# A new slot order for the attention stacks, with merged rotary products

## The reference, cut to what matters

```python
for i in range(DEPTH):                                    # 6
    x = attn_layer(shift_tokens(x), Wqkv[i], ...) + x
    x = ffn_layer(shift_tokens(x), ln_g[i], ...) + x
# attn_layer: 16 heads of 64, window 32
q, k, v = split(x @ Wqkv)
q = l2norm(q) * qs;  k = l2norm(k) * ksc
q = q * cos * scale + rotate_half(q) * sin * scale        # k with 1 / scale
sim = einsum(q, k of this window and the one before) * 8; masked
out = softmax(sim) @ v;  out @ Wo
# ffn_layer: layer norm, a * gelu(gate) @ W2 + b2, inner width 341
```

## Time and profile before

| | us |
|---|---|
| median of 3 runs | 4334.24 (4328.81 to 4348.74) |
| profiled execution | 4352.9 |
| its span in the profile | 4351.2 |
| TensorE busy | 4027.8 (93%) |
| VectorE busy | 3345.6 (77%) |
| ScalarE busy | 3100.0 (71%) |
| GpSimd busy | 1798.7 (41%) |
| mean of one factor (L835) | 1.469 |
| mean of one addition (L841) | 2.364 |
| mean of one exponential (L1143) | 0.363 |

### The profile page before, as it was taken

One profiled execution on the slowest core, in us unless ns is written; L12 is line 12 of the kernel. 1 busy time (PEld: TensorE's weight loads), 2 busy tenths in 40 slices (PEclk: granted clock), 3 DMA queues, 4 the chain that ended last, 5 costly groups with the idle time before them and its releaser, 6 DMA issues. The chain is left out here.

```text
span 4351.2 us, 113662 instructions
## 1 busy us (share of the span) xinstructions
PE 4027.8 (93%) x43857; PEld 2388.8 (55%) x43857; DVE 3345.6 (77%) x4981; ACT 3100.0 (71%) x7032; POOL 1798.7 (41%) x1071
## 2 busy tenths in 40 slices
PE   7997999999999999999967689999999999999998
PEld 3443555555555555555536545555555555555554
DVE  5774888888888888888735478888888888888885
ACT  3555777777777777777762267777777778777776
POOL 3111444444444444444404534444444444444442
PEclk7997999999999999999986589999999999999999
DMA  2212444444443443444300044444434444444342
GB/s 44 31 21 70 95 111 102 99 101 101 105 111 90 111 107 90 111 99 103 84 10 3 3 107 109 101 97 109 110 87 115 102 100 100 102 105 111 92 100 52
DMA packets 232520, 380.78 MB, mean 88 GB/s; under 512 B 59364, under 2 KB 122336, under 8 KB 231688
## 3 DMA queue, kind: packets, MB, share of 16 engines
q1 hardware_dynamic: 231560, 372.20, 36.9%
q10 hardware_dynamic: 384, 0.79, 0.1%
HBM read 39.22 MB, written 1.05 MB: 9 GB/s over the span
## 5 line engine op out<-in xcount | busy, mean ns | idle before, releaser
L835 POOL TENSOR_TENSOR b_prob<-b_prob,b_rinv 128x768 f32<-128x768 f32 x384 | 564.3, 1469 | 1778.3 <-DVE b_rinv L1281 1778.3
L841 POOL TENSOR_TENSOR b_prc<-b_prc,b_sws 128x1024 f32<-128x1024 f32 x384 | 907.7, 2364 | 72.2 <-DMA b_sws<-b_prs 72.2
L1143 ACT ACTIVATE b_prob<-ps,b_nmx 128x96 f32<-128x96 f32 x3072 | 749.0, 363 | 0.0
L885 PEld LDWEIGHTS ps<-ident,b_prob 128*128 128x128 f32 x3072 | 367.9, 140 | 406.5 <-ACT b_pT L1079 232.8
L1216 DVE SCALAR_TENSOR_TENSOR b_prc<-ps,b_qks,b_rot 128x512 f32<-128x512 f32 x768 | 571.1, 744 | 14.0 <-ACT b_sq L1104 13.3
L1218 DVE SCALAR_TENSOR_TENSOR b_prs<-ps,b_qks,b_rot 128x512 f32<-128x512 f32 x768 | 570.1, 742 | 0.0
L885 PE MATMUL ps<-ident,b_prob 128*128 128x128 f32 x3072 | 513.0, 281 | 46.5 <-DVE b_kr L1264 37.1
L1262 DVE TENSOR_TENSOR b_prc<-b_prc,ps 128x512 f32<-128x512 f32 x384 | 263.6, 686 | 369.9 <-PE ps L950 288.3
L1079 ACT ACTIVATE b_pT<-ps 128x512 f32<-128x512 f32 x724 | 435.5, 601 | 154.1 <-PE ps L885 151.1
L987 PE MATMUL ps<-b_wqkv,b_xs 128*128 128x256 f32 x1536 | 435.0, 406 | 2.2 <-DVE b_prs L1218 2.2
L938 PE MATMUL ps<-b_xs,b_wqkv 128*128 128x512 f32 x768 | 408.9, 614 | 23.3 <-issue 10.0
(11 more groups left out here) (293 smaller groups left out, 7218.0 us busy)
## 6 DMA issues: line engine op xcount, KB each, us to landing
b_sws<-b_prs SPq DMA_DIRECT2D x1536, 128.0 KB, 2.3
b_vs<-b_va SPq DMA_DIRECT2D x384, 256.0 KB, 3.8
b_wqkv<-in_L_ffn_Wqkv SPq DMA_DIRECT2D x96, 192.0 KB, 3.6
b_xs<-y SPq DMA_DIRECT2D x126, 128.0 KB, 2.3
b_wo<-in_L_ffn_Wo SPq DMA_DIRECT2D x96, 64.0 KB, 3.1
b_xs<-y SPq DMA_DIRECT2D x42, 127.8 KB, 2.4
b_rot<-in_rot SPq DMA_DIRECT2D x2, 2048.0 KB, 7.8
b_w<-in_L_ffn_W SPq DMA_DIRECT2D x24, 170.5 KB
```

The lines of the kernel that those rows point to most:

```text
L835: pool.tensor_tensor(prob[:, r, :, P - KEYS:P], prob[:, r, :, P - KEYS:P], rinv[:, r % 2, :].rearrange("p (b a) -> p b a", a=1).broadcast_ ...
L841: pool.tensor_tensor(prc[:, r, :, :], prc[:, r, :, :], sws[:, r % 2, :, :], ALU.add)\
L885: t = pe.transpose(bank[6][:, i * P:(i + 1) * P], prob[:, kd, 4 * e + 2 * h + m, :], ident[:, :])
L1143: g = act.activation(prob[:, kb, i, P - KEYS:P], wide[0][:, e * CH + m * KEYS:e * CH + (m + 1) * KEYS], ACT.Exp, bias=nmx[:, kb % 2, i:i + 1])
```

## The change

The order of the instructions of a slot is written anew for TensorE, ScalarE, VectorE and GpSimd; SyncE's stays. The special order after a gelu goes. Banks: the spreads use 1 and 2 (so the key projection waits for L1262, which empties bank 1), the strips bank 6, the output projection bank 7, mean, variance and gates bank 2, hidden and output products bank 3.

TensorE's slot becomes: first transposition (after the factor of its unit), output projection of the unit of age 5, spreads, query, hidden or output product of the feed-forward part, key, second transposition, mask and scores, strips (odd), values, mean, variance or gate, value projection. A `sem_inc` on a semaphore that nobody waits for is put ahead of mask and scores. GpSimd adds before it multiplies by the factor. VectorE starts a slot with the rotary products of the unit before, each pair of products one instruction; `prc`, `prs` and `kr` become parts of one tensor for that.

```diff
+        roll = sb("roll", [P, 12 * CH + PAD + T])
+        prc = roll[:, 0:8 * CH].rearrange("p (r i c) -> p r i c", r=4, i=2)
+        prs = roll[:, 8 * CH:12 * CH].rearrange("p (r i c) -> p r i c", r=2, i=2)
+        kr = roll[:, 12 * CH:12 * CH + PAD + T]
+        def two_runs(first, second):
+            return bass.AP(roll[:, :].tensor, first, [roll[:, :].ap[0], [second - first, 2], [1, CH]])
 # GpSimd
-                    if u: ... wait rinv_done ... pn_done      (the factor, moved down)
                     if v:
                         pool.wait_ge(S["swap_ld"], ONE + 64 * (U + 1))
                         ... add ... .then_inc(S["add_done"], 1)
+                    if u: ... wait rinv_done ... pn_done
 # TensorE, slot
+                    if d:
+                        pe.wait_ge(S["pn_done"], ONE + UD + 1)
+                        if p and j % 2 == 0:
+                            pe.wait_ge(S["ln_done"], ONE + twos(p) + 1)
+                        turn(UD, kd, 0)
+                    if e:
+                        pe.wait_ge(S["o_cp"], ONE + UE + 1)
+                        pe.matmul(bank[7], wo[:, pair(e), :], oT[:, ke % 2, :], ...).then_inc(S["wo_mm"], 1)
+                    if b:
+                        pe.wait_ge(S["split_done"], ONE + twos(b) + 1)
+                        if p:
+                            pe.wait_ge(S["pk_done"], ONE + um(p)[0] + 1)
+                        pe.matmul(bank[1][:, :], take[:, 2 * (kb % 2), :], rsp[:, :], ...)
+                        key_bank_free(f0)
+                        pe.matmul(bank[2][:, :], take[:, 2 * (kb % 2) + 1, :], rsp[:, :], ...).then_inc(S["nb_mm"], 1)
                     if a: ... query projection, behind va_cp ...
+                    hidden_bank_free(f0)
+                    ... hidden product (f_in) or output product (f_hid) into bank[3] ...
+                    if a:
+                        if b:
+                            pe.wait_ge(S["qn_done"], ONE + UB + 1)
+                        pe.matmul(bank[1][:, :], W[:, 1, :], X, ...).then_inc(S["k_mm"], 1)
+                    if d:
+                        turn(UD, kd, 1)
                     if b:
+                        pe.wait_ge(S["exp_done"], ONE + UB)
+                        pe.wait_ge(S["kn_done"], ONE + UB + 1)
+                        pe.sem_inc(S["s_go"], 1)
                         mask(kb) ... scores
+                    if a and j % 2:
+                        strips(U, d)               # waits sqk_done of U, pt_cp of both halves
                     if d:
                         values(d, 0)
                         values(d, 1)
+                    ... mean, variance or gate into bank[2], behind kn_done ...
                     if a: ... value projection, behind sqq_done and pq_done ...
 # ScalarE, slot: copy of output (e); square of step 1; variance or gate copy; copy of values (p);
 #   first transposition; affine of step 2; table load; exponentials (age 3); square of query;
 #   second transposition; table load and gelu (step 5); square of key; inverse norms (odd)
+                    if d:
+                        turned(1)
                     if step == 5:
                         act.preload_act_table_set("gelu_and_others")
                         act.wait_ge(S["f_gcp"], ONE + FT * C + FT)
                         act.activation(gel, gel, ACT.Gelu).then_inc(S["f_gelu"], 1)
+                    if a:
+                        act.wait_ge(S["k_mm"], ONE + U + 1)
+                        act.activation(sq[:, 2 * (r % 2) + 1, :], bank[1][:, :], ACT.Square).then_inc(S["sqk_done"], 1)
+                        if j % 2:
+                            inverse_norms(twos(a))
 # VectorE
-                    dve.scalar_tensor_tensor(out=prc[:, r, i, :], in0=bank[i][:, :], scalar=scale,
-                                             in1=rot[:, 2 * i, t], op0=ALU.mult, op1=ALU.mult)
-                    dve.scalar_tensor_tensor(out=prs[:, r % 2, i, :], in0=bank[i][:, :], scalar=scale,
-                                             in1=rot[:, 2 * i + 1, t], op0=ALU.mult, op1=ALU.mult).then_inc(S[done], 1)
+                    both = bank[i][:, :].rearrange("p (a c) -> p a c", a=1).broadcast_to([P, 2, CH])
+                    dve.scalar_tensor_tensor(out=two_runs((2 * r + i) * CH, (8 + 2 * (r % 2) + i) * CH), in0=both, scalar=scale,
+                                             in1=rot[:, 2 * i:2 * i + 2, t], op0=ALU.mult, op1=ALU.mult).then_inc(S[done], 1)
 # VectorE, slot: products of p (query, key); maximum (age 3); norm of step 2; centring; hidden copy;
 #   y of the feed-forward part; split (even); query rows (b); y (e); key rows (b); sum and reciprocal (age 3)
```

More of the change, by code:

```diff
@@ new lines, in slot @@
+                    if ok is not None:
+                        pe.wait_ge(S["f_hid"], ONE + OC + 1)
+                        for i in range(FT):
+                            m = pe.matmul(bank[3][:, :], w2[:, i, :], hid[:, i, :], start=(i == 0), stop=(i == FT - 1))
+                        m.then_inc(S["f_out"], 1)
+                    if a:
+                        if b:
+                            pe.wait_ge(S["qn_done"], ONE + UB + 1)
+                        elif p:
+                            pe.wait_ge(S["pk_done"], ONE + um(p)[0] + 1)
+                        pe.matmul(bank[1][:, :], W[:, 1, :], X, start=True, stop=True).then_inc(S["k_mm"], 1)
@@ L952, in slot @@
-                    if d and before != 5:
-                        turn(UD, kd, 0)
-                    key_bank_free(f0)
-                    if a:
-                        pe.wait_ge(S["pk_done"], ONE + U)
-                        pe.matmul(bank[1][:, :], W[:, 1, :], X, start=True, stop=True).then_inc(S["k_mm"], 1)
-                    if d and before == 5:
-                        turn(UD, kd, 1, b)
-                    if d and before != 5:
-                        turn(UD, kd, 1, b)
-                    if a and j % 2 and before != 5:
-                        strips(U, b)
@@ L989, in slot @@
                         m.then_inc(S["va_mm"], 1)
-                    if a and j % 2 and before == 5:
-                        strips(U, b)
-                    if d:
-                        if isinstance(d[0], int) and d[0] == 0:
-                            pe.wait_ge(S["wo_ld"], ONE + 16 * PAIRS * (L0 + 1))
-                        elif d[1] < HALF and d[1] % 2 == 0:
-                            pe.wait_ge(S["wo_ld"], ONE + 16 * (PAIRS * (L0 + d[0]) + pair(d) + 1))
-                        pe.wait_ge(S["o_cp"], ONE + UD + 1)
-                        if not b:
-                            pe.wait_ge(S["kn_done"], ONE + PER * (L0 + DEPTH))
-                        pe.wait_ge(S["y_add"], ONE + UD)
-                        pe.matmul(bank[3][:, :], wo[:, pair(d), :], oT[:, kd % 2, :], start=True, stop=True).then_inc(S["wo_mm"], 1)
@@ L1225, in slot @@
                     ok, OC = ffn_out(f0)
-                    follows = before in (0, 2, 4) or ok is not None
-                    if b and j % 2 == 0 and not follows:
-                        n = twos(b)
-                        dve.wait_ge(S["rn_done"], ONE + n + 1)
-                        dve.scalar_tensor_tensor(out=rsp[:, :], in0=rhi[:, :].bitcast(F32), scalar=minus_hi[:, 0:1], in1=rn[:, :],
-                                                 op0=ALU.mult, op1=ALU.add).then_inc(S["split_done"], 1)
```

278 lines of the change are left out of this document (122 added, 156 removed).

## The result

The changed kernel takes 4398.61 us, median of 4 runs (4395.76 to 4404.53), beside 4341.49 for the kernel before (4328.81 to 4351.09, 4 runs; the forecast was put on the 4334.24 of three): ratio 1.0135, 95% interval 1.0102 to 1.0168. It is 57 us slower, where 47 was forecast. The profiled execution spans 4402.8 us against 4351.2.

The account below looks back on a forecast made before the run. TensorE, busy 4027.8 of 4351.2 us, was taken as the bound; 22 half layers at 2.4 us more, less 2 x 3, gave 47 us on the 4334.24 median: 4381 us, range 4260 to 4465.

Parts of the forecast that it names:

- The sum: Slots 0 to 15 added up to 149.2 against 146.8 us; over all half layers 47 us slower, 4381 us.
- The layout: New order timed, slot by slot: plain odd slot 8.65 us, even 7.3, slots 0 to 15 together 149.0.
- rival 5: Merged rotary products read the repeated operand at half rate, adding 1.1 us a slot on VectorE: 4490 us, chance 4%.
- The chain over GpSimd: Key's product, DMAs, addition, then factor gate the next slot's first transposition: 8.3 us, which just fits TensorE's 16.6 a pair.
- rival 3: GpSimd's factor behind its addition binds if the DMA landing takes over 4.3 us: 107 us slower, 4441 us, chance 13%.
- rival 4: VectorE's split meets GpSimd's addition, 1.0 us in even slots: 4430 us with a quarter met, 4560 with all; chance 5%.
- Rival 1: Key's square is done when scores end, so odd-slot strips don't stall: 4298 us, or 4256 with free gelu slots; 25%.
- Rival 2: No change: gelu slots cost what they do now, the rest stays: 5 us slower, 4339 us, chance 17%.
- the value projection waits for the first product: In slots 0, 2, 8, 14 it waits 0.1 to 0.6 us for the rotary product, 1.1 us together.
- 9.18 us a slot, so 146.8 us for 16 slots: Base for the old order: mean over 191 slots of the first stack, taken as the time of half a layer.
- +2.4: Extra time of a half layer with a feed-forward part in the new order, 149.2 against 146.8 us, counted 22 times.
- On the path it is worth something only where the value projection waits: Merging the rotary products saves VectorE 0.25 us a slot, mostly slack, useful only where the value projection awaits the first product.

Follow-up runs that it names:

- e2: Changed kernel with the layer loops of all engines written out, no branch: 4351.0 us, ratio 1.0017.
- e8: Changed kernel, all loops written out, with four edits (spreads before output projection, key's square before gelu, strips between value products, feed-forward output behind values): 4362.97 us, ratio 1.0046.
- e3: Kernel before the change with the layer loops of all engines written out: 4341.16 us, ratio 0.9993.
- e4: Changed kernel with its loops, each merged rotary product split back into two 512-wide instructions: 4407.48 us, ratio 1.0136.
- e11: Kernel before the change in its own order, all loops written out, only the two products of each rotary pair merged: 4314.16 us, ratio 0.9937.
- e1: Changed kernel with VectorE's rotary products moved to the end of its slot, ahead of the loop's branch, same instruction sequence: 4396.32 us, ratio 1.0122.
- e5: Changed kernel with the layer loop written out for TensorE alone: 4379.17 us, ratio 1.0088.
- e6: Changed kernel with the layer loop written out for TensorE and ScalarE: 4383.33 us, ratio 1.0101.
- e10: Changed kernel with the layer loop written out on VectorE, GpSimd and SyncE, kept on TensorE and ScalarE: 4393.28 us, ratio 1.0113.
- e9: Changed kernel, all loops written out, with odd-slot spreads ahead of the output projection and strips between the two value products: 4374.86 us, ratio 1.007.

## Why the prediction was right, and where it was not

*The sum.* Forecast +47, measured +57. The sign was right for the order itself, which costs 10 us written out. That the size came so near is luck: two errors cancel, an order that was priced too high and a loop that was not priced at all.

*The layout* was right: 149.0 a half layer, each slot within 0.1 us. Some 0.9 of the 149.0 go with the loop, though: the same slots take 148.1 in written-out code (e2), where a strip waits 0.23 instead of 0.30. The strips wait 0.30 against 0.25 and the cold start of 0.1; the output projection and slots 8 and 9 as laid out. Merged product 1.278 against 1.28, so rival 5 falls. The chain over GpSimd holds the first transposition 11.9 us in all, so it "just fits", and rival 3 falls. The split takes 0.760 on average against 1.264 before, so rival 4 falls for this order; e8 shows its price. Rival 1 needed the strips not to stall; they stall 190 times. Rival 2 needed the gelu slots to cost what they had cost, 19.4 for slots 8 and 9; they took 20.7. One term was too large: the value projection waits for the first product 2.8 us in all, not 1.1 a half layer.

*"9.18 us a slot, so 146.8 us for 16 slots"* is the step that failed. It is the mean of unlike halves and was set against a layout of the ordinary one, which takes 148.0. The forecast's +2.4 was +1.0. With the short halves (the first of each stack, not the last as the prediction has it), where the forecast took off 3 and the runs show 5, the order would have given +12; written out, the runs say +10.

*What was missing* is the layer loop: 44 to 47 us of the 57, shown by e2 and e3, nearly all of it (45 by the slots) at the eight branches back. No term, rival or sign in the prediction had it, though the trace of before has its idle row too (1.69 us of weight load at 3105.38). The layout began each slot with an engine whose next instruction is at hand.

*"On the path it is worth something only where the value projection waits"*, of the merge, holds in the new order as far as e4 can tell, and was not asked of the old one, where it is wrong: e11 has 27 us where that wait was 2.2. The variance product waited for the key's rotary product in the trace of before too, and gives 11 of the 27. Put together from medians: merge written out -27, new order +37 (e2 against e11; 35 by the ratios), loops 47 in the new order against 3 in the old: 54 of the measured 57. That the new order costs 37 beside a merged old one, and another 44 with the loops, is why the change doesn't pay.

*Open.* Why the new order is so open to the branch. What was shown: it isn't where VectorE's slot is cut (e1), and no one engine's. What was only argued: in the old order the last instructions of TensorE's slot 31 are the six matmuls of the feed-forward output, 2.7 us of work in one piece, while in the new one a value projection of 1.1 us, behind waits, is last, so the branch is reached late. No run put a block of queued work ahead of the branch.

## What to carry to other kernels

Lay out a slot by hand from starts in one trace: here it held to 0.1 us. But set it against slots of the same kind, never against a mean over a stage, and look at the loop's last slot by itself: "issue" idle time at the first instruction behind a branch, on any engine in a ring, is a term of the sum. To find what a shorter instruction is worth, list everyone who waits for it, not only the product that comes to mind. A stall on the path is a saving only if what stands behind it is ready, so move one at a time and read the next row.

## What the runs showed of the hardware

- At the branch back of the layer loop the first instruction behind it stood idle 3.0 to 3.3 us on VectorE, 1.9 to 2.9 on ScalarE and 2.5 to 3.5 on TensorE (changed kernel, e1, e5, e6, e10), with nothing else in the profile holding it; in e1, where VectorE's products stand ahead of the branch, its idle time was 1.7 to 2.0. In e2, without the branch, none of this is there. The price depends on the order: by the slots, 45 us at eight branches in one order and 12 in the other. The Trainium skill ("Advanced Engine Details and Errata", Sequencer and Instruction Queues) gives a branch some 51 to 108 ns; the idle times here are 16 to 32 times the larger figure. The same section says that an engine holds only two cache lines of its instructions; a fetch of the loop's start would fit the gap, but no run measured it by itself.
- After 2.5 to 3.1 us without a matmul at the eight branches of the changed kernel, TensorE's granted clock was 1.2 GHz for 3.4 to 10.2 us at seven of them and stayed at 2.4 at one (2.57 us); TensorE had worked 23.6 of 24 us shortly before. After the 44 waits of 1.85 us in e9 (slots 9 and 15) it fell for 3.4 us 12 times, at 1.7 us each.
- A scalar_tensor_tensor that reads one PSUM bank twice through a repeated axis took 1.278 us for 1024 columns, as long as a plain one of 1024 (1.281), where two of 512 take 1.40 from the first's start to the second's end.
- A VectorE instruction with two SBUF inputs that begins 0.5 us after a GpSimd addition of 2.35 us took 2.38 us instead of 0.75 (e8).
